# Four tiles in flight, first FFN five tiles ahead, inputs turned by DMA, search steps on GpSimd

## What is computed

```python
x = x + 0.5 * ffn(layernorm(x), A, B, Wr)
x = x + mlp(layernorm(x), w_gate, w_up, w_down)
x = x + 0.5 * ffn(layernorm(x), A, B, Wr)
# ffn: scores = x @ Wr.T; G = softmax over the top 16 of 64, else 0
#      out = ((x @ A_k) * G_k) @ B_k, summed over k, * 2
# mlp: s = silu(x @ w_gate.T); the 688 of 1376 with smallest |s| become 0
#      out = (s * (x @ w_up.T)) @ w_down.T
```

## Time and profile before

| | us |
|---|---|
| median of 3 runs (897.61 to 902.42) | 898.3 |
| profiled execution | 900.5 |
| its span, first to last instruction | 898.5 |
| PE busy | 753.2 (84%) |
| DVE busy | 571.4 (64%) |
| ACT busy | 360.9 (40%) |
| POOL busy | 36.3 (4%) |

### The profile page before, as it was taken

The page is one execution under the profiler, slowest core; times in us unless marked ns, Lnnn a source line. Parts: engine busy times, 40 slices in busy tenths (PEclk is TensorE's granted clock), DMA queues, the critical chain, the costliest instruction groups (busy, mean ns, idle before and its releaser), DMA issues.

```text
span 898.5 us, 10482 instructions
## 1 busy us (share of the span) xinstructions
PE 753.2 (84%) x3863; PEld 356.3 (40%) x3863; DVE 571.4 (64%) x1403; ACT 360.9 (40%) x449; POOL 36.3 (4%) x104
## 2 busy tenths in 40 slices
PE   2766570999999898999999999999989999985555
PEld 0322230454545454444444444444444545442122
DVE  5355547576767676768686767676775767663521
ACT  4235574434343434343434343434434353433100
POOL 0000000000000000000000000000000000000000
PEclk9977795899999999999999999999999999997777
DMA  6332100213131313131312121212221221212121
GB/s 216 127 137 81 57 1 6 51 24 79 24 80 24 80 24 80 24 80 24 79 25 68 34 61 33 68 36 68 36 68 24 54 49 40 53 34 34 24 44 35
DMA packets 118922, 49.17 MB, mean 55 GB/s; under 512 B 110832, under 2 KB 110832, under 8 KB 118864
## 3 DMA queue, kind: packets, MB, share of 16 engines
q1 hardware_dynamic: 118864, 48.45, 22.8%
HBM read 16.97 MB, written 4.19 MB: 24 GB/s over the span
## 4 chain that ended last, share of the span: by engine, by line
PE 74%; DVE 10%; DMA 6%; issue 4%; ACT 4%; SPq 2%; DVEq 0%; POOL 0%; POOLq 0%; ACTq 0%
PE ps L351 24%; PE ps L352 23%; PE ps L353 23%; DMA vt_hi<-stage 3%; PE ps L378 2%; DVE xt_lo L702 1%; ACT xt_hi L535 1%; DMA pt_lo<-stage 1%; DMA stage<-w_a 1%; DMA vt_lo<-stage 1%; DVE y L931 1%; DVE w_d_lo L685 1%; PE ps L364 1%; ACT signs L554 1%; DVE small L655 1%
## 5 line engine op out<-in xcount | busy, mean ns | idle before, releaser
L554 ACT ACTIVATE signs<-mag,small 128x1376 bf16<-128x1376 f32 x112 | 161.4, 1441 | 144.8 <-DVE small L759 141.6
L351 PE MATMUL ps<-w_b_hi,pt_hi 128*128 128x512 f16 x256 | 100.0, 391 | 24.1 <-DMA pt_lo<-stage 16.5
L351 PE MATMUL ps<-w_d_hi,vt_hi 128*128 128x512 f16 x176 | 68.8, 391 | 38.3 <-issue 24.2
L351 PE MATMUL ps<-w_a_hi,xt_hi 128*128 128x512 f16 x256 | 100.3, 392 | 0.0
L352 PE MATMUL ps<-w_a_hi,xt_lo 128*128 128x512 f16 x256 | 100.0, 391 | 0.0
L352 PE MATMUL ps<-w_b_hi,pt_lo 128*128 128x512 f16 x256 | 99.9, 390 | 0.0
L353 PE MATMUL ps<-w_b_lo,pt_hi 128*128 128x512 f16 x256 | 99.7, 389 | 0.0
L353 PE MATMUL ps<-w_a_lo,xt_hi 128*128 128x512 f16 x256 | 99.6, 389 | 0.0
L351 PE MATMUL ps<-w_g_hi,xt_hi 128*128 128x512 f16 (+1 forms) x192 | 69.3, 361 | 8.7 <-DVE w_g_lo L685 6.1
L351 PE MATMUL ps<-w_u_hi,xt_hi 128*128 128x512 f16 (+1 forms) x192 | 69.4, 361 | 6.5 <-DVE w_u_lo L685 6.1
L352 PE MATMUL ps<-w_g_hi,xt_lo 128*128 128x512 f16 (+1 forms) x192 | 69.5, 362 | 0.0
(11 more groups left out here) (115 smaller groups left out, 1186.9 us busy)
## 6 DMA issues: line engine op xcount, KB each, us to landing
xin<-x SPq DMA_DIRECT2D x16, 256.0 KB, 3.0
out<-y SPq DMA_DIRECT2D x16, 256.0 KB, 2.0
stage<-w_g SPq DMA_DIRECT2D x4, 688.0 KB, 5.9
stage<-w_u SPq DMA_DIRECT2D x4, 688.0 KB, 5.9
stage<-w_d SPq DMA_DIRECT2D x5, 512.0 KB, 6.2
stage<-w_a SPq DMA_DIRECT2D x4, 512.0 KB, 7.2
stage<-w_b SPq DMA_DIRECT2D x4, 512.0 KB, 9.2
pt_hi<-stage SPq DMA_TRANSPOSE x30, 3.2
```

The source lines that it names most:

```text
L351: pe.matmul(dst, x_hi, w_hi, start=start, stop=False)
L554: act.activation(signs[:, :], mag[1 - b][:, :], ACT.Sign, bias=thr, scale=-1.0, accum_out=bal).then_inc(counted, 1)
```

## The change

Work of four tiles stands side by side. Iteration `d` (from -1 to 15) does down and FFN 3 of tile d, search, select, mask and up of tile d+1, gate, `tanh`, `silu` and `magnitude` of tile d+2, the second norm of tile d+3 and FFN 1 of tile d+5, of which x was normed an iteration before. In the last five iterations (`first(d)` is None) there is no FFN 1. x lives in nine slots and is updated in place. `combine` has a PSUM bank of its own, `down` another; gate and up share one set of banks, so `ups(t)` waits for `silu(t)` and `gates(t+1)` for `gated(t)`.

All inputs are turned by DMA. `x_to_hi` and `x_to_lo` write both halves side by side in SBUF, and one transpose turns both; the same for the expert values and the MLP values. TensorE's transposes are gone.

The search steps move from VectorE to GpSimd: six instructions in place of four, and `aim` for the first threshold. `mark` is gone: `select` works out the flag from its eight candidates in four small instructions, TensorE sums it over the rows (`sum_flags`), and `check` reads one value. GpSimd also loads B, G, U and D (the other weights stay with SP) and makes the low halves of two pieces of G, two of U and three of D, with two instructions a piece. `mask` is one instruction over magnitudes and values.

```diff
+LEAD = 4
+SLOTS = 9
...
+MG = Matrix("g", DC, I, 1, P, AT_G, 2, (1, 3))
+MU = Matrix("u", DC, I, 1, P, 0, 2, (1, 3))
+MD = Matrix("d", IC, D, 2, LAST, AT_G, 0, (1, 3, 5))
...
+calls = [(1, t) for t in range(LEAD + 1)]
+for d in range(NT):
+    calls += [(1, d + LEAD + 1)] if d + LEAD + 1 < NT else []
+    calls += [(3, d)]
+number = {c: k for k, c in enumerate(calls)}
...
+        def turn_x(j, t):
+            sp.wait_ge(x_hi_ready[j], t + 1)
+            sp.wait_ge(x_lo_ready[j], t + 1)
...
+            sp.dma_start_transpose(dst[:, :, :], halves[j]).then_inc(xt_loaded[j], 16)
...
+        def turn_v(t):
+            if t >= 1:
+                sp.wait_ge(down_done, t)
+            sp.wait_ge(v_hi_ready, t + 1)
+            sp.wait_ge(v_lo_ready, t + 1)
+            sp.dma_start_transpose(vt, v_both).then_inc(vt_loaded, 16)
...
+        def split_lo(m, n):
+            c, k, rows = m.pieces[n]
+            w = staged(m, c, k, rows)
+            pool.wait_ge(w_hi_made, pieces_before(m) + n + 1)
+            link(pool.tensor_scalar(w, w, scale[m.name][0:rows, :], None, ALU.mult))
+            pool.tensor_tensor(lo[m.name][0:rows, c:c + k, :], w, hi[m.name][0:rows, c:c + k, :],
+                               ALU.subtract).then_inc(w_lo_pool, 1)
...
+        def aim(t):
+            pool.wait_ge(mag_ready, t + 1)
+            link(pool.tensor_scalar(step, mag_sum, -SPACING / 2, None, ALU.mult))
+            pool.tensor_scalar(thr, mag_sum, GUESS, None, ALU.mult).then_inc(thr_ready, 1)
+        def search(t, n):
+            pool.wait_ge(counted, ROUNDS * t + n + 1)
+            link(pool.tensor_scalar(off, bal, -7.0, None, ALU.add))
+            link(pool.tensor_scalar(far, off, off, 7.5 ** 2, ALU.mult, ALU.is_gt))
+            link(pool.tensor_tensor(move, off, far, ALU.mult))
+            link(pool.tensor_tensor(move, move, step, ALU.mult))
+            link(pool.tensor_scalar(move, move, DAMP[n], None, ALU.mult))
+            pool.wait_ge(thr_ready, ROUNDS * t + n + 1)
+            pool.tensor_tensor(thr, thr, move, ALU.add).then_inc(thr_ready, 1)
+        def emit(d):
+            f = first(d)
+            for n in range(ROUNDS - 1):
+                if n == 3 and d >= 0:
+                    rstd(3, d)
+                if d + 1 < NT:
+                    search(d + 1, n)
+            if f is not None and f + 1 < NT:
+                rstd(1, f + 1)
+            if d + 3 < NT:
+                rstd(2, d + 3)
+            if d + 2 < NT:
+                aim(d + 2)
...
+        pool.wait_ge(w_loaded["a"][1], 16)
+        for n in range(len(MB.pieces)):
+            load_w(MB, n)
+        rstd(1, 1)
+        for n in range(len(MG.pieces)):
+            load_w(MG, n)
...
+        for n in MD.by_pool:
+            split_lo(MD, n)
...
-        def turn_x(j, t):
-            pe.wait_ge(normed_ready[j], t + 1)
-            for c in range(DC):
-                mm = pe.transpose(bank(0, P, c * P), normed[j][:, c * P:(c + 1) * P],
-                                  ident[:, :])
-            mm.then_inc(xt_turned[j], 1)
...
+        def experts(j, t, fresh=False):
+            k = number[j, t]
...
+            if k:
+                pe.wait_ge(routed_ready, k)
...
+        def ups(t, fresh=False):
+            pe.wait_ge(gate_ready, t + 1)
...
+        def down(t):
+            if t == 0:
+                split_done(MD, IC - 1)
+            else:
+                pe.wait_ge(x2_ready, t)
+            pe.wait_ge(vt_loaded, 16 * (t + 1))
...
+        def sum_flags(t):
+            if t:
+                pe.wait_ge(x2_ready, t)
+            pe.wait_ge(flag_ready, t + 1)
+            pe.matmul(bank(DOWN, 1), ones[:, :], flag[:, 0:1], start=True, stop=True
...
+        def emit(d):
+            f = first(d)
+            if d >= 0:
+                down(d)
+            if f is not None:
+                experts(1, f)
+            if d == -1:
+                norms(MD)
+            if d + 1 < NT:
+                ups(d + 1, d == -1)
+            if f is not None:
+                if d >= 0:
+                    experts(3, d)
+                sum_flags(d + 1)
+                combine(1, f)
+                if d + 2 < NT:
+                    gates(d + 2)
             else:
-                turn_x(3, i - 2)
...
+                combine(3, d - 1)
+                if d + 2 < NT:
+                    gates(d + 2)
+                if d + 1 < NT:
+                    sum_flags(d + 1)
+                experts(3, d)
+            if d >= 0 and not late(d):
+                combine(3, d)
+        pe.wait_ge(const_made, 2)
+        norms(MR)
+        norms(MA)
+        experts(1, 0, fresh=True)
+        experts(1, 1)
+        norms(MB)
+        experts(1, 2)
+        combine(1, 0, fresh=True)
+        norms(MG)
+        experts(1, 3)
+        combine(1, 1)
+        pe.wait_ge(scale_made, 4)
+        norms(MU)
+        combine(1, 2)
+        pe.wait_ge(scale_made, 5)
+        gates(0, fresh=True)
+        combine(1, 3)
+        for d in range(-1, NT):
+            emit(d)
+        combine(3, NT - 1)
...
+        def emit(d):
+            f = first(d)
+            def median(*rounds):
+                if d + 1 < NT:
+                    for n in rounds:
+                        count(d + 1, n)
+            median(0, 1, 2, 3)
+            if f is not None:
+                exps(number[1, f])
+            if d >= 0:
+                x_to_hi(3, d)
+            if f is not None:
+                median(4, 5)
+                p_to_hi(number[1, f])
+                median(6)
+                if d >= 0:
+                    exps(number[3, d])
+                    p_to_hi(number[3, d])
+                v_to_hi(d + 1)
+                if f + 1 < NT:
+                    x_to_hi(1, f + 1)
+                x_to_hi(2, d + 3)
+                tanh(d + 2)
+                magnitude(d + 2)
+            else:
+                median(4, 5, 6)
+                if d + 1 < NT:
+                    v_to_hi(d + 1)
+                if d + 2 < NT:
+                    tanh(d + 2)
+                    magnitude(d + 2)
+                exps(number[3, d])
+                p_to_hi(number[3, d])
+                if d + 3 < NT:
+                    x_to_hi(2, d + 3)
...
-        def search(i, n):
...
-            link(dve.tensor_scalar(off, bal, -7.0, None, ALU.add))
-            link(dve.tensor_scalar(far, off, off, 7.5 ** 2, ALU.mult, ALU.is_gt))
-            link(dve.scalar_tensor_tensor(out=move, in0=off, scalar=far, in1=step,
-                                          op0=ALU.mult, op1=ALU.mult))
-            dve.scalar_tensor_tensor(out=thr, in0=move, scalar=DAMP[n], in1=thr,
-                                     op0=ALU.mult, op1=ALU.add).then_inc(thr_ready, 1)
...
+        def select(t):
+            dve.wait_ge(counted, ROUNDS * (t + 1))
+            if t:
+                dve.wait_ge(v_hi_ready, t)
+                dve.wait_ge(v_lo_ready, t)
+            link(dve.scalar_tensor_tensor(out=masked[:, 0:I], in0=mag, scalar=thr, in1=mag,
+                                          op0=ALU.is_le, op1=ALU.mult))
+            link(dve.max(cand8, masked[:, 0:I]))
+            link(dve.scalar_tensor_tensor(out=top_a, in0=evens, scalar=bal, in1=cand8,
+                                          op0=ALU.is_equal, op1=ALU.mult, accum_out=kth))
+            link(dve.tensor_scalar(greater, cand8, kth, None, ALU.is_gt, ALU.add,
+                                   accum_out=above))
+            link(dve.scalar_tensor_tensor(out=wrong, in0=above, scalar=2.0, in1=bal,
+                                          op0=ALU.mult, op1=ALU.not_equal))
+            link(dve.scalar_tensor_tensor(out=wrong, in0=bal, scalar=15.0, in1=wrong,
+                                          op0=ALU.is_gt, op1=ALU.max))
+            if t:
+                dve.wait_ge(flag_summed, t)
+            dve.scalar_tensor_tensor(out=flag[:, 0:1], in0=cand8[:, 0:1], scalar=thr,
+                                     in1=wrong, op0=ALU.is_equal, op1=ALU.max
+                                     ).then_inc(flag_ready, 1)
+        def mask(t):
...
-            bad = [dve.value_load(flagged[q:q + 1, :], min_val=0, max_val=1)
-                   for q in range(0, P, 32)]
-            with dve.If(bad[0] + bad[1] + bad[2] + bad[3] != 0):
-                bisect(m)
...
+        def check(t):
+            dve.wait_ge(flag_summed, t + 1)
+            link(dve.tensor_copy(flagged, bank(DOWN, 1)))
+            bad = dve.value_load(flagged[0:1, :], min_val=0, max_val=P)
+            with dve.If(bad != 0):
+                bisect()
+            dve.memset(spare[:, 4:5], 0.0).then_inc(masked_ready, 1)
...
+        def emit(d):
+            f = first(d)
+            if f is not None:
+                k1 = number[1, f]
+                if d >= 0:
+                    k3 = number[3, d]
+                    if d >= 1:
+                        add_ffn(3, d - 1)
+                    add_down(d)
+                    norm_stats(3, d)
```

(161 more changed lines are left out.)

988 lines of the change are left out of this document (377 added, 611 removed).

## The result

The changed kernel takes 950.75 us (median of 4 runs, 949.40 to 954.96) against 897.95 for the kernel before in the same comparison: ratio 1.0586, 95% interval 1.0536 to 1.0635. 912 was predicted, with 868 to 965 as the range: slower, as said, but by 5.9% where the forecast was 1.5%.

What follows compares the result with a forecast made beforehand. TensorE bounds the kernel now; afterwards the closed search loop does, 49.4 us a turn. First select 138, intervals 713.4 and end 60.3 sum to 911.7, so 912 us (+1.5%), range 868 to 965.

Steps and rivals of the forecast that it cites:

- the closed loop of the search: Counts, select, silu, magnitude and aim chain into the next tile's counts, one turn per tile: 49.4 us, above TensorE's 42.8.
- 21.9 in the working: Search part of a turn: six rounds of 3.39 us (20.3) and a seventh count of 1.6; bounds 20.8 to 27.3.
- 4.6 + 9.2 + 5.6 + 8.1 = 27.5: VectorE's list in a turn: select 4.6, choose to check 9.2, v halves to rstd 5.6, norm_apply to aim 8.1 us.
- 1.72 was taken: Six GpSimd instructions of one search step: three at 0.27 us, three two-input ones at 0.33; bounds 1.54 and 2.62.
- a rival of 1.9 us with chance 0.12: Shared port: p_to_lo (1.2) and x_to_lo (0.7) hold GpSimd's search up in 11 turns, 933 us; chance 0.12.
- 138 as an estimate; bounds 128 and 150: Time of the first select, in us, from laying the start's lists one behind the other; 143.0 before the change.
- 61.7 - 4 + 2.7 + 1.3: End after the last select: mark and loads go, x turned by DMA, p and v in one transfer; given as 60.3 us.
- Cheap steps: Rival: one-column GpSimd search steps cost less than their 0.27 us spacing; time near 865 us, chance 0.20.
- Dear steps: Rival: two-input GpSimd search steps cost what the power costs, 0.9 us a round more; 993 us, half 950; chance 0.17.
- The overlap works as drawn: Rival: the loop isn't closed and TensorE sets 42.8 us a tile; about 835 us, chance 0.05.
- a wait for the flag of some 4 us: Sign for the prediction: TensorE waits for VectorE's flag before sum_flags, some 4 us a tile.
- a first `select` past 150: Sign against the prediction: the start's first select later than 150 us, where 138 was estimated.

Runs made afterwards that it cites:

- run 3: Changed kernel with a search step in four GpSimd instructions instead of six, same values: 922.61 us, ratio 1.0253.
- run 4: Changed kernel with the search steps back on VectorE, four instructions placed between its other work: 860.45 us, ratio 0.9590.
- run 8: Changed kernel with VectorE's low halves of p(k1) and of x of tile three held until no search step runs on GpSimd: 932.58 us, ratio 1.0356.
- run 1: Changed kernel with all low halves of G, U and D made on VectorE, none on GpSimd: 928.69 us, ratio 1.0334.
- run 11: Changed kernel with one line moved: on GpSimd, rstd of tile 0's second norm ahead of its two pieces of G: 944.90 us.
- run 13: Changed kernel, search still on GpSimd, all low halves on VectorE, two held off the search steps, U loaded behind the transposes: 909.66 us, ratio 1.0097.
- run 5: Changed kernel with the search steps and the low halves of all weight pieces both on VectorE: 845.72 us, ratio 0.9383.
- run 12: Changed kernel with search steps and all low halves on VectorE and U's load issued after tile 3's turned operand landed: 835.70 us, ratio 0.9311.
- the late load: U's load held back until x of tile 3 has been turned; on the changed kernel alone 947.33 us, 3.4 us back.
- run 2: Changed kernel with U's load held back until x of tile 3 is turned, and that tile's rstd ahead of it: 947.33 us, ratio 1.0532.

## Why the prediction was wrong in size

*What bounds before and after: right.* TensorE was the bound and the closed loop of the search took its place (runs 3 and 4); TensorE's own work per tile, 42.8 in the working, is 42.9 in run 4.

*The turn: its terms were right, one was left out.* From the first count (442.43) to `select` (465.89) are 23.46 us in the changed kernel against 21.9 in the working; in run 8, with the low halves held back, it is 430.88 to 452.77, 21.89. From `select` to the next tile's first count (493.03) follow 27.1 us against 4.6 + 9.2 + 5.6 + 8.1 = 27.5. The steps cost 1.73 us, where 1.72 was taken; in that sum the two-input steps were priced too high (0.33 against 0.27) and the others too low (0.27 against 0.31 to 0.38). What was left out is the engines' mutual hold, 0.55 + 1.01 = 1.56 us in this turn and 1.43 in the mean of the ten: it stood as a rival of 1.9 us with chance 0.12 and belonged into the sum, since in this code both low halves fall on search steps in every full turn. The prediction says that `p_to_lo` becomes an instruction with two SBUF inputs; it was one already (L717, `routed,stage`), and what is new is that search steps run on GpSimd beside it. The 15 intervals are 725.4 against 713.4, 12.0 of the miss; run 8 gives 18.2 us back in median, and 14.5 of them are the ten full turns.

*The start: the step that failed.* "Laying the lists one behind the other ... I get 138 as an estimate; bounds 128 and 150." It was 166, outside the bounds the text itself set, and 28 of the 38 us of the profiled miss. The text says that a wide step on GpSimd has no row and gives that as the reason for its bounds, but states no price for one, neither in the estimate nor in the bounds. Measured are 6.6 us for a piece of G, 6.6 and 8.5 for the two of U and 14.1 for the three of D, where VectorE needs 1.64 for one of the largest (run 1). The text named that VectorE waits for `rstd` and that D's pieces stand ahead of the first search step, but priced neither: 19.9 us of VectorE's standing (5.9 of it on the path, run 11) and 9.1 us of ScalarE's wait for the first search step. Runs 1 and 13, without GpSimd's pieces, put the first `select` at 141.3 and 142.3, so the rest of the laying out was some 4 us off, which is within the chance that run 5 shows.

*The end: near, with an error in the sum.* 58.6 us against 60.3. The terms named, 61.7 - 4 + 2.7 + 1.3, add up to 61.7 and not to 60.3, so nothing that the text names gives the 3.1 us that the end became shorter. No run takes it apart.

*The rivals.* "Cheap steps" fell: the three two-input steps are 0.19 us long, but the next starts 0.27 after each, as in the earlier trace rows; of the others two take 0.21 and the one with a column as scalar 0.30. "Dear steps" fell too. "The overlap works as drawn" came to 835 by its working, and run 12, once the search is off GpSimd and the start is mended, takes 835.7. That the two agree is chance: the start is 8.6 us shorter than in that rival's sum (129.4 against 138) and the intervals are some 9.5 longer (645.3 against 636).

*Signs named ahead.* Intervals of 49 (50.4), rounds of 3.4 (3.37), a wait for the flag of some 4 us (60.6 us in 12 places, 5.1 each) came as said; so did the one that was to prove the prediction wrong, a first `select` past 150.

## What to carry to other kernels

Before a chain is moved to an idle engine, count how often it is passed: two short instructions less in a step gave 28 us back, over 96 rounds of a closed loop. The whole move, with steps 0.9 us longer, the held steps and the queue at the start, cost 90 us in the new order and 35 in the old one. An engine that is idle in the profile of before has no row for wide operations; until there is one, the sum has to carry a wide bound for it (here it was the largest miss), and everything that stands behind it in its queue (a small norm step, the first step of a search) pays it too. What a small edit to the start is worth can't be told from one "first" when chance alone moves it by 8 us; the late load gave 3.4, 10.0 and about 1 us beside different edits.

## What the runs showed of the hardware

GpSimd took 3.76 us for a 128x1376 multiplication by a column and 2.79 for a subtraction of two inputs; VectorE makes both in one instruction of 1.64 (run 1). Undisturbed, the one-column steps of the search took 0.19 to 0.30 us on GpSimd and started 0.27 to 0.38 apart. VectorE's operations are stretched by GpSimd as well as the other way: 0.55 became 4.01 (a norm, with one wide input) beside a multiplication of 3.76, and 0.69 became 3.28 beside a subtraction of 3.40. The transpose of p(1) took 1.93 us of queue time in run 2 and 6.97 (run 8) to 12.82 (run 5) where 2.8 MB of U's load were issued about 1 us ahead of it. In the changed kernel it landed 17.4 us after its issue:

```profile
pt<-p_both SPq DMA_TRANSPOSE x1, 17.4
```
